# Cross attention of a Perceiver block: mixes issued four chunks at a time, six places for E, output weights loaded later

## The reference

```python
Q = _proj(query, Wq, bq)          # 256 x 512, 16 heads of 32
K = _proj(key, Wk, bk)            # 25088 x 512, from the context
V = _proj(value, Wv, bv)          # 25088 x 512, from the context
scores = jnp.einsum('bihd,bjhd->bijh', Q, K) * SCALE
attn = jax.nn.softmax(scores, axis=1)
x = jnp.einsum('bijh,bjhd->bihd', attn, V).reshape(B, S, D_MODEL)
return x @ Wo + bo
```

## Time and profile before

| | |
|---|---|
| median of 3 runs | 2837.94 us (2837.16 to 2838.08) |
| profiled execution | 2838.73 us |
| its span in the profile | 2836.7 us |
| PE busy | 2709.4 us, 96% of the span |
| ACT busy | 2007.3 us, 71% |
| DVE busy | 1964.3 us, 69% |
| POOL busy | 838.1 us, 30% |
| mean granted TensorE clock | 0.98 |

### The profile page before, as it was taken

How to read it: one execution, slowest core, us unless ns; L and a number is a source line. 1 busy time by engine, 2 the same in 40 slices (tenths; PEclk the granted TensorE clock), 3 DMA queues, 4 the chain that set the end, 5 groups by cost and what they waited for, 6 DMA issues and landing times.

```text
span 2836.7 us, 58540 instructions
## 1 busy us (share of the span) xinstructions
PE 2709.4 (96%) x21096; PEld 2220.2 (78%) x21096; DVE 1964.3 (69%) x3785; ACT 2007.3 (71%) x7206; POOL 838.1 (30%) x1151
## 2 busy tenths in 40 slices
PE   7997799999999999999999999999999997799998
PEld 5775699877877778778777787777777875599997
DVE  6774667567777777777777777777777773555555
ACT  2111344279999999999999999999999992345543
POOL 4431111123333333333333333333333322122222
PEclk9998899999999999999999999999999998899999
DMA  8983345366666666666666566666656552355441
GB/s 338 391 309 145 110 180 196 123 161 152 159 151 151 164 157 157 153 158 154 152 160 151 148 164 157 157 156 159 153 152 160 144 123 90 128 183 197 184 178 67
DMA packets 132147, 473.26 MB, mean 167 GB/s; under 512 B 31112, under 2 KB 31240, under 8 KB 124688
## 3 DMA queue, kind: packets, MB, share of 16 engines
q1 hardware_dynamic: 131856, 469.52, 57.1%
HBM read 244.47 MB, written 17.30 MB: 92 GB/s over the span
## 4 chain that ended last, share of the span: by engine, by line
PE 84%; DVE 6%; POOL 5%; issue 2%; DMA 2%; ACT 1%; SPq 0%; POOLq 0%; DVEq 0%
PE PB L526 18%; PE PB L551 14%; PE PB L559 12%; PE PB L539 11%; PE PB L619 7%; PE PB L635 6%; PE PB L487 5%; PE PB L389 5%; POOL CTX L1310 3%; PE PB L500 2%; DVE small L1069 2%; POOL VS L1321 1%; PE PB L412 1%; DMA AR<-in_ctx 1%; DVE V L1065 1%
## 5 line engine op out<-in xcount | busy, mean ns | idle before, releaser
L750 ACT ACTIVATE EE<-PB,small 128x256 f32<-128x256 f32 x3136 | 1446.0, 482 | 131.9 <-DVE small L1069 118.2
L1069 DVE TENSOR_REDUCE small<-PB 128x2 f32<-128x512 f32 x1568 | 1063.5, 679 | 439.4 <-PE PB L551 438.9
L1321 POOL TENSOR_TENSOR VS<-V,small 128x128 f32<-128x128 f32 x784 | 348.3, 444 | 1206.9 <-DVE small L1075 1206.9
L750 ACT ACTIVATION_READ_ACCUMULATOR EE<-PB,small 128x1 f32 x3136 | 663.8, 212 | 0.0
L551 PEld LDWEIGHTS PB<-QS,STK 128*128 128x128 f32 x3136 | 480.5, 190 | 202.7 <-issue 163.8
L526 PE MATMUL PB<-CTX,WKV 128*128 128x256 f32 x4704 | 624.9, 282 | 3.6 <-DVE CTX L1050 2.6
L551 PE MATMUL PB<-QS,STK 128*128 128x256 f32 x3136 | 605.6, 295 | 6.5 <-issue 3.2
L526 PEld LDWEIGHTS PB<-CTX,WKV 128*128 128x128 f32 x4704 | 588.7, 190 | 4.4 <-DVE CTX L1050 3.1
L559 PE MATMUL PB<-EE,VS 128*32 128x256 f32 x6272 | 426.6, 386 | 8.4 <-POOL VS L1321 8.4
L539 PE MATMUL PB<-WKV,CTX 128*128 128x512 f32 x1584 | 432.5, 395 | 0.8 <-DVE V L1065 0.8
L539 PEld LDWEIGHTS PB<-WKV,CTX 128*128 128x128 f32 x1584 | 273.0, 190 | 37.0 <-DVE V L1065 1.2
(11 more groups left out here) (198 smaller groups left out, 2248.2 us busy)
## 6 DMA issues: line engine op xcount, KB each, us to landing
STK<-KHL SPq DMA_DIRECT2D x1568, 128.0 KB, 2.9
RW<-in_l1f SPq DMA_DIRECT2D x32, 2048.0 KB, 8.1
AR<-in_ctx SPq DMA_DIRECT2D x49, 1024.0 KB, 8.2
RAW<-in_ctx SPq DMA_DIRECT2D x98, 512.0 KB, 4.2
WF<-in_l0f SPq DMA_DIRECT2D x17, 2304.0 KB, 8.7
v_scr<-RAW SPq DMA_DIRECT2D x64, 256.0 KB, 8.0
V<-v_scr SPq DMA_DIRECT2D x64, 256.0 KB, 2.9
WA<-in_l0a SPq DMA_DIRECT2D x1, 4096.0 KB, 12.6
```

Source lines behind the costliest of these rows:

```text
L750: m = e.activation(EE[:, b, s, :], bank(2 * (k % 2) + half, 256 * (s % 2), 256), ACT.Exp, bias=nm[:, b, s:s + 1], accum_out=su[:, b, s:s + 1])
L1069: e.tensor_reduce(nm[:, k % 4, 2 * half:2 * half + 2], bank(2 * (k % 2) + half).rearrange("p (s i) -> p s i", s=2), axis=AX.X, op=ALU.max, ...
L1321: e.tensor_tensor(VS[:, b, :].rearrange("p (s d) -> p s d", s=4), V[:, t % 4, 128 * c:128 * c + 128].rearrange("p (s d) -> p s d", s=4), r ...
```

## The change

1. `MIX = 4`: PE mixes after every fourth chunk. After chunk k with k % 4 = 3 it mixes chunks k - 5, k - 4, k - 3 and k - 2 in one row (after chunk 3 only chunks 0 and 1). After the loop's last chunk the last two are mixed as before.
2. `RING = 6`: EE and VS have six places, and so have the maxima, sums and reciprocals. `exps(k)` waits for `mix(k - 6)` in place of `mix(k - 4)`.
3. QHL, the split Q, no longer has space of its own: WO lies over it. So WO is loaded later: no more ahead of the loop, but in SP's loop at k = 40, behind a wait for the 16 DMAs that read QHL.

```diff
+MIX = 4
+RING = 6
...
-        VS = sb("VS", [P, 4, P], over=life)
-        EE = sb("EE", [P, 4, 4, 256], over=life)
+        VS = sb("VS", [P, RING, P], over=life)
+        EE = sb("EE", [P, RING, 4, 256], over=life)
         OT = sb("OT", [P, NC, 256], over=life)
+        q_life = ExitStack()
+        QHL = sb("QHL", [P, 2, NC, 256], F32R, q_life)
+        q_life.close()
         WO = sb("WO", [P, NC, D], over=life)
-        QHL = sb("QHL", [P, 2, NC, 256], F32R, life)
...
             e.dma_start(wqx, a["l1x"][:, 0:2048].rearrange("p (c n) -> p c n", c=NC)).then_inc(S["d_wx"], 16)
-            e.dma_start(WO[:, :, :], a["l1x"][:, 2048:4096].rearrange("p (c n) -> p c n", c=NC)).then_inc(S["d_wo"], 16)
...
                 if k % 8 == 5 and g + 6 < NG:
                     load_ctx(g + 6)
+                if k == 40:
+                    w.wait_ge("d_q", 256)
+                    e.dma_start(WO[:, :, :], a["l1x"][:, 2048:4096].rearrange("p (c n) -> p c n", c=NC)).then_inc(S["d_wo"], 16)
...
             def mix(k):
-                t, c, b = k // 4, k % 4, k % 4
+                t, c, b = k // 4, k % 4, k % RING
...
                 scores(k, 1)
-                if k % 2 and k >= 3:
-                    mix(k - 3)
-                    mix(k - 2)
+                if k % MIX == MIX - 1:
+                    for n in range(max(k - MIX - 1, 0), k - 1):
+                        mix(n)
...
             def exps(k, half):
-                b = k % 4
+                b = k % RING
                 w.wait_ge("s_max", 2 * k + half + 1)
-                if k >= 4:
-                    w.wait_ge("mix_mm", k - 3)
+                if k >= RING:
+                    w.wait_ge("mix_mm", k - RING + 1)
```

More of the change, by code:

```diff
@@ L216, in build @@
         qf = EE[:, 3].rearrange("p c i -> p (c i)")
-        nm = small[:, 0:16].rearrange("p (b s) -> p b s", b=4)
-        su = small[:, 16:32].rearrange("p (b s) -> p b s", b=4)
-        rc = small[:, 32:48].rearrange("p (b s) -> p b s", b=4)
+        nm, su, rc = (small[:, o:o + 4 * RING].rearrange("p (b s) -> p b s", b=RING) for o in (0, 32, 64))
         KBANK = (6, 2, 3, 4)
@@ L1069, in maxima @@
                 e.tensor_reduce(
-                    nm[:, k % 4, 2 * half:2 * half + 2], bank(2 * (k % 2) + half).rearrange("p (s i) -> p s i", s=2),
+                    nm[:, k % RING, 2 * half:2 * half + 2], bank(2 * (k % 2) + half).rearrange("p (s i) -> p s i", s=2),
                     axis=AX.X, op=ALU.max, negate=True).then_inc(S["s_max"], 1)
@@ L1074, in reciprocals @@
                 w.wait_ge("s_exp", 2 * k + 2)
-                e.reciprocal(rc[:, k % 4, :], su[:, k % 4, :]).then_inc(S["s_rcp"], 1)
+                e.reciprocal(rc[:, k % RING, :], su[:, k % RING, :]).then_inc(S["s_rcp"], 1)
             split_hi(0)
@@ L1314, in scale_v @@
             def scale_v(k):
-                b, t, c = k % 4, k // 4, k % 4
+                b, t, c = k % RING, k // 4, k % 4
                 w.wait_ge("s_rcp", k + 1)
```

## The result

| | us |
|---|---|
| before, median of 4 runs | 2837.62 (2837.16 to 2838.08) |
| changed, median of 4 runs | 2857.09 (2853.98 to 2858.36) |
| ratio | 1.0067, 95% interval 1.0050 to 1.0084 |
| changed, profiled execution | 2856.93, span 2854.9 |

The change costs 19.5 us (0.7%), clear of the noise. The prediction was 2860 us, 3 too many, with the range from 2836 to 2873.

What follows compares the result with a forecast made beforehand. PE was taken to set the pace. Each of 192 blocks loses 0.33 us and gains 0.46, net +0.136, or 26 us; less 4 for scale_v waits gives +22, so 2860 us, range 2836 to 2873.

Steps and rivals of the forecast that it cites:

- Item 1: PE's mixes: one group of four replaces two of two, saving one passage, 0.33 us a block.
- Item 2: Second pair's project_k: waits for k_lo, which the first pair's mixes had covered; 0.46 us late a block.
- rival B: Passage saved and project_k doesn't wait for k_lo: faster, 2762 to 2775 us; chance 0.12.
- Item 3: Mix waiting for POOL's scale_v in 32 blocks: 0.40 goes and 0.28 comes, -4 us together.
- Item 4: ACT's exps with six places: no new wait, ACT idles 0.6 us a block unfelt by PE; cost 0.
- Item 5: WO loaded in the loop: no gain at the front, cost 0, at most a late K stack under 3 us.
- Item 6: Last 16 chunks, ACT-bound: four mixes fit beside the exps ACT still holds; cost 0 within 1 us.
- Rival A: The forecast: project_k waits for k_lo in every second pair; 2860 us, range 2850 to 2872; chance 0.75.
- C: project_k waits, but weights load ahead of the wait and restart costs nothing: no change, 2840 us; chance 0.11.
- D: PE's wait in each block lowers the granted clock: much slower, possibly hundreds of us; chance 0.02.

Runs made afterwards that it cites:

- the run of the rest alone: Changed kernel with MIX = 2, keeping six places for E and VS and the output weights loaded at k = 40: 2838.46 us, ratio 0.9998.
- one swap on DVE: Changed kernel, four mixes, with DVE issuing k_lo ahead of maxima(k, 0) of the next chunk, not behind it: 2796.82 us, ratio 0.9852.

## Why the prediction was right

- **Item 1, the saved passage (-0.33 a block).** Right: 0.32 for one passage more in the kernel with single mixes, and the block of 8.68 where no wait is left (9.01 - 8.68 = 0.33).
- **Item 2, the lost cover (+0.46).** Right: 0.45. k_lo's end at 3.96, plus 0.06, plus 0.10 came as 3.95, 0.06 and 0.10. The net was put at +0.136 a block and is +0.12, which is the 3 us between forecast and result. Two details were off. The waits were to add up to 60 to 70 us for PE, about 0.35 each. The starts are 0.35 late, but the view has 0.20 each, 37.7 us in all, and 0.40 each for the weight loads, since it counts from modelled ends. And the limit for rival B (k_lo's end at 3.53 to 3.60) was set a little late: PE is held from 3.50 on.
- **Item 3, the wait for VS (0.40 goes, 0.28 comes).** Right: long blocks take 0.27 more than the others, so 0.40 goes and 0.27 comes, 4 us less over the 32. With the +0.12 these blocks come out at 9.40, next to 9.42 before.
- **Item 4, ACT.** Right for this kernel: ACT idles 0.44 ahead of a block's first exps (I said 0.6), and no matmul of PE waits for it in the loop. The experiments show how near it was: with six mixes, or a DVE order that makes ACT wait, it decides.
- **Item 5, WO.** Right, by the run of the rest alone.
- **Item 6, the end.** That run has two mixes and says nothing of it; the traces do. The net cost is -0.8 us from the last project_k to the end, as forecast, but two parts cancel that the item didn't have. The stretch to the last mix takes 2.8 us more (39.0, not 36.2): behind waits of PE for ACT of 0.4 to 0.7 us the granted clock falls to its lower level there, and its mean is 0.91, where it was 0.99. Before, the fall came behind the last mix, in the product with WO: that took 10.1 us at a mean of 0.59 and now takes 7.1 at 1.00. The agreement of this item is luck in part.
- **Rival A** was the case. **Rival B** had the right mechanism for what one swap on DVE gives, but I priced it wrong: 2762 to 2775, where the swap alone gives 2797. I let the wait for VS vanish with it; in truth the mixes come 0.46 earlier then, and that wait grows from 34 places to 97 over the whole run. With the group's rounding moved as well 2762 comes out. **C** (weights loaded past the wait) is ruled out by the rows of the restart, 1.53 in place of 1.43 behind each wait. **D** did not happen: in the loop the granted clock stays at 1.00 with an idle PE in every block.

## What to carry to other kernels

Before work is gathered into larger groups, ask what the scattered pieces were covering: here the mixes between two projections gave the evacuation of a single-buffered PSUM bank 1.18 us (4.84 against 3.66), and 0.88 of them were slack. Without them the saving of 0.33 was smaller than the wait of 0.45 laid bare. The remedy is not to give up the grouping but to shorten the chain that has lost its cover, by the order on the engine that evacuates, and only where it lost it: an early wait holds up what stands behind it in its engine's order. After each such step the next wait (here VS on POOL) has to be priced again, since the whole schedule has moved.

## What the runs showed of the hardware

- A passage from 128-column matmuls to 32-column ones and back costs 0.32 to 0.33 us, the same whether a group has 8, 16 or 32 instructions of mixes (pairs of 4.83 and 4.51, blocks of 9.01 and 8.68).
- A restart of PE after a wait that has let it run dry costs 0.10 us beyond the wait itself (12 matmuls and their successors 1.53 in place of 1.43 us), at full clock. The same 0.10 is lost, with no idle matmul in the view, where the operation waited for ends only 0.06 ahead of the matmul's own start, and none of it where it ends 0.22 to 0.30 ahead.
- Idle times of about 0.9 us of PE in every block of 9.9 us did not lower the granted clock (1.00 from 600 to 2300 us of the run with the late k_lo; 0.981 over that run, 0.980 before).
